# Two expert layers computed for the chosen experts alone, and attention worked in octets of half a sequence

## What is computed

```
x = x + 0.5 * ffn(LN(x))        # token-shift layer: mixes each row with the row before
x = x + attention(LN(x))        # 8 heads, softmax over 1024 keys, values wide
x = x + 0.5 * ffn(LN(x))
x = x + 0.5 * experts(LN(x))    # 16 experts, each token uses its best 2
x = x + linear_attention(LN(x)) # decaying state, scanned over the sequence
x = x + 0.5 * experts(LN(x))    # same weights again
```

```
probs = softmax(x_flat @ Wr + br)
topk_w, topk_idx = top_k(probs, 2);  topk_w /= sum(topk_w)
h   = x_flat @ W1[e] + b1[e]                      # 128 -> 128, for each expert e
h   = gelu(layernorm(h) * g1[e] + be1[e])
out = h @ W2[e] + b2[e]                           # 128 -> 128
y   = sum over the two chosen experts of topk_w * out
```

## Time and profile before

| | us |
|---|---|
| median of three runs | 894.28 |
| span of the profiled execution | 895.7 |
| PE busy (matmul) | 757.8 (85%) |
| DVE busy | 755.3 (84%) |
| ACT busy | 480.5 (54%) |
| POOL busy | 271.6 (30%) |

### The profile page before, as it was taken

The page is one execution under the profiler, slowest core; times in us unless marked ns, Lnnn a source line. Parts: engine busy times, 40 slices in busy tenths (PEclk is TensorE's granted clock), DMA queues, the critical chain, the costliest instruction groups (busy, mean ns, idle before and its releaser), DMA issues.

```text
span 895.7 us, 12505 instructions
## 1 busy us (share of the span) xinstructions
PE 757.8 (85%) x4069; PEld 408.9 (46%) x4074; DVE 755.3 (84%) x1697; ACT 480.5 (54%) x1245; POOL 271.6 (30%) x229
## 2 busy tenths in 40 slices
PE   4846889999999988998989896846989989989966
PEld 2523112232322333556656566624543556656656
DVE  7996799888887558799999999578764898999995
ACT  1424005767676876765766563335116765667742
POOL 4020000000000001234455456655000244456557
PEclk7788557999999998998999999976997999999998
DMA  7006860000000000000000000000000000000000
GB/s 235 1 3 138 179 104 2 1 1 2 1 1 2 1 0 1 1 1 1 1 0 2 0 1 1 1 1 0 2 1 1 0 2 12 1 1 13 1 12 13
DMA packets 11793, 16.66 MB, mean 19 GB/s; under 512 B 1456, under 2 KB 5584, under 8 KB 11728
## 3 DMA queue, kind: packets, MB, share of 16 engines
q1 hardware_dynamic: 11728, 15.86, 7.7%
HBM read 11.55 MB, written 4.19 MB: 18 GB/s over the span
## 4 chain that ended last, share of the span: by engine, by line
DVE 37%; PE 17%; issue 7%; ACT 6%; POOL 3%; POOLq 0%; DVEq 0%; ACTq 0%
DVE arena L1010 7%; DVE arena L994 6%; DVE small L206 6%; PE ps L854 3%; DVE arena L206 3%; POOL x L1089 3%; DVE small L202 3%; ACT arena L695 2%; PE ps L876 2%; DVE arena L1327 2%; PE ps L1209 1%; PE ps L579 1%; PE ps L1140 1%; DVE stat L215 1%; PE ps L853 1%
## 5 line engine op out<-in xcount | busy, mean ns | idle before, releaser
L1089 POOL TENSOR_TENSOR x<-x,arena 128x512 f32<-128x512 f32 x136 | 208.8, 1535 | 291.5 <-DVE arena L1010 288.0
L695 ACT ACTIVATE arena<-ps 128x512 f32<-128x512 f32 x256 | 132.4, 606 | 101.9 <-PE ps L568 101.7
L629 DVE TENSOR_REDUCE arena<-ps 128x1 f32<-128x512 f32 x256 | 159.5, 681 | 23.6 <-PE ps L549 23.0
L876 PE MATMUL ps<-w,arena 128*128 128x128 f32 x1024 | 141.1, 282 | 13.7 <-DVE arena L1010 9.2
L854 PE MATMUL ps<-w,xt 128*128 128x512 f32 x256 | 151.5, 675 | 0.0
L930 ACT ACTIVATE arena<-ps 128x512 f32<-128x512 f32 x128 | 76.4, 597 | 126.8 <-PE ps L854 107.7
L876 PEld LDWEIGHTS ps<-w,arena 128*128 128x128 f32 x1024 | 127.8, 196 | 18.5 <-ACT arena L968 10.0
L549 PE MATMUL ps<-arena 96*128 96x512 bf16 x256 | 112.3, 451 | 12.3 <-DMA arena<-att_parts 10.7
L968 ACT ACTIVATE arena<-ps,w 128x512 f32<-128x512 f32 x128 | 101.2, 791 | 31.5 <-PE ps L864 31.4
L864 PEld LDWEIGHTS ps<-cst,arena 128*128 128x128 f32 x512 | 63.4, 144 | 90.3 <-issue 45.4
L864 PE MATMUL ps<-cst,arena 128*128 128x128 f32 x512 | 80.2, 280 | 28.1 <-DVE arena L994 27.9
(11 more groups left out here) (181 smaller groups left out, 958.2 us busy)
## 6 DMA issues: line engine op xcount, KB each, us to landing
arena<-att_parts SPq DMA_DIRECT2D x28, 128.0 KB, 8.2
att_parts<-arena SPq DMA_DIRECT2D x12, 256.0 KB
arena<-att_parts SPq DMA_DIRECT2D x4, 384.0 KB, 8.8
x<-in_x SPq DMA_DIRECT2D x4, 256.0 KB, 3.5
arena<-att_parts SPq DMA_DIRECT2D x4, 256.0 KB, 9.4
out_x<-x SPq DMA_DIRECT2D x4, 256.0 KB, 2.3
w<-in_wpack SPq DMA_DIRECT2D x1, 611.0 KB, 5.8
row<-in_rows SPq DMA_DIRECT2D x1, 592.0 KB, 8.0
```

Of the source, the lines that this page charges most:

```text
L629: nc.vector.tensor_reduce(a_nm[:, hd % 2, k % 2, k // 2:k // 2 + 1], ps[:, RING_BANKS[u % 3], :], AX.X, ALU.max, negate=True).then_inc(a.m ...
L695: nc.scalar.activation(a_p[:, v % 8, half * 512:(half + 1) * 512], ps[:, score_bank(unit), :], ACT.Exp, scale=0.25).then_inc(a.ex, 1)
L876: ins = pe.matmul(ps[:, 4 + v % 2, j * P:(j + 1) * P], m_a[:, u % 4, j * P:(j + 1) * P], w2[:, 4 * (s % 4) + e, :], start=True, stop=True)
L1089: nc.gpsimd.tensor_tensor(xq, xq, m_tmp[:, v % 4, :].rearrange("p (j o) -> p j o", j=4), ALU.add)\
```

## The change

- **Expert layers.** The dense layer is replaced. Per half: DVE finds for each row its two experts as before, counts with two PE products and running sums how many rows go to each expert, and gives every (row, choice) a slot in a table of rows sorted by expert, each expert's part rounded up to whole tiles of 128 rows. With 2048 (row, choice) pairs in 16 experts, 31 tiles (NTL) always suffice, and 31 are always computed. POOL scatters the normalised rows into that table in DRAM with 16 indirect transfers of 128 rows; SP loads the table back in 8 groups of up to four tiles (31 = 7 x 4 + 3); each tile is transposed, multiplied with its expert's W1, scaled, transposed, passed through gelu and multiplied with W2, where the weights' address comes from a register that PE loads from a table of tiles; ACT starts the transfers of the results to DRAM; POOL gathers them back with 16 indirect transfers of 128 rows per half; DVE adds them to x with the gates.
- Biases go through DRAM (`bias_parts`), one more indirect transfer per half and three by SP; SP clears the two tables during attention.
- **Attention by octets.** An octet is a quad's four heads for half of the queries; the order of the ring, the maxima, the transfers of them (four per octet, 32 in all, 16 before) and the outputs go by octet. 42 ring units precede the first score.
- The norm statistics of the ffn layer of half 0 go between the ring's units in attention.
- PE runs products of zeros (`keep_clock`) while DVE routes.

```
-        RING_FIRST = turn_at[3] + 1 + 4
-        RING_SLOTS = 190
+        for o in range(NO):
+            for k in range(32):
+                ring.append(("mp", o, k))
+                if k == TURN_AFTER and o:
+                    ring.append(("turn", o - 1, 0))
...
+        RING_FIRST = turn_at[0] + 4
+        RING_OVER = 212
...
+            for o in range(first, last):
+                b, h0, half = octet(o)
+                sp.wait_ge(a.mpu, turn_at[o] + 1)
+                for k in range(NQ):
+                    sp.dma_start(a_qs[96:99, b, h0 + k, 512 * half:512 * (half + 1)].rearrange("i (j s) -> i j s", j=4),
+                                 a_nmt[12 * k:12 * k + 12, o % 2, :]).then_inc(a.nmrow[o], 16)
...
+            def scores(n):
+                o, i, h4 = n // 32, n % 32 // 4, n % 4
+                b, h0, half = octet(o)
+                if n % 32 == 0:
+                    pe.wait_ge(a.nmrow[o], 16 * NQ)
...
+        NTL = 2 * S // P + NE - 1
+        NGR = (NTL + 3) // 4
+        LEAD = 3
...
+        def moe_vector_slots(dve, vs, m):
...
+            yield vs.mark(nc.vector.tensor_tensor_scan(r_run[:, 8:8 + P], ps[:, bank, P:2 * P], zerof[:, 0:P], 0.0,
+                                                       ALU.add, ALU.add))
+            yield vs.mark(nc.vector.scalar_tensor_tensor(out=r_n, in0=ends, scalar=P - 1.0, in1=before, op0=ALU.add,
+                                                         op1=ALU.subtract))
...
+            nc.vector.tensor_copy(r_slot[b], r_slotf).then_inc(m.slot, 1)
...
+        def moe_pool_send(pool, m):
...
+            pool.wait_ge(m.slot, m.i + 1)
+            pool.wait_ge(s_clean, 32 * B)
+            for k in range(2):
+                for j in range(TB):
+                    pool.indirect_dma_start(
+                        out=rows_in[b], out_offset=bass.IndirectOffsetOnAxis(ap=r_slot[b][:, k * TB + j:k * TB + j + 1], axis=0),
+                        in_=xl[:, TB * b + j, :], in_offset=None).then_inc(m.sent, 16)
+                if k == 0:
+                    moe_pool_bias(pool, m)
...
+        def moe_pool_fetch(pool, m):
+            b, i = m.b, m.i
+            for k in range(4):
+                pool.wait_ge(t.ys[k], 16 * 2 * (i + 1))
+            for q in range(4):
...
+                for j in (2 * q, 2 * q + 1):
+                    for k in range(2):
+                        pool.indirect_dma_start(
+                            out=t_yg[:, b, k, j, :], out_offset=None, in_=rows_out[b],
+                            in_offset=bass.IndirectOffsetOnAxis(ap=r_slot[b][:, k * TB + j:k * TB + j + 1], axis=0))\
+                            .then_inc(t.yg[q], 16)
...
+        def moe_sync_load(sp, m, g):
+            b, u = m.b, NGR * m.i + g
+            if g == 0:
+                sp.wait_ge(m.sent, m.all_sent)
...
+            def hidden(u):
+                m, g = pair[(u - u0) // NGR], (u - u0) % NGR
...
+                regs = [pe.alloc_register(f"e{u}_{j}") for j in range(4)]
+                pe.load(regs, r_tab[m.b][0:1, 4 * g:4 * g + 4])
+                at = [pe.snap(r, min_val=0, max_val=(NE - 1) * P) for r in regs]
...
+                pe.matmul(ps[:, bank, :], pick[:, g, :], brow[:, m.b, :, 0, :], start=True, stop=False)
+                for j in range(k):
+                    ins = pe.matmul(ps[:, bank, j * P:(j + 1) * P], t_xt[:, u % 2, j * P:(j + 1) * P],
+                                    w1[:, :, :].rearrange("c e f -> c (e f)")[:, bass.ds(at[j], P)], start=False, stop=(j == k - 1))
...
+            routed(pair[0])
+            turn_in(u0)
+            for u in range(u0, u0 + LEAD):
+                turn_in(u + 1)
+                hidden(u)
+                between(u - u0)
+            routed(pair[1])
+            for u in range(u0, last):
+                turn(u)
+                if u + LEAD + 1 < last:
+                    turn_in(u + LEAD + 1)
+                if u + LEAD < last:
+                    hidden(u + LEAD)
+                out(u)
...
+            for u in range(u0, last):
+                gelu(u)
+                if u > u0:
+                    store(u - 1)
+                if u + LEAD + 1 < last:
+                    rows(u + LEAD + 1)
+                if u + LEAD < last:
+                    squares(u + LEAD)
+                out_in(u)
+            store(last - 1)
...
+            for u in range(u0, u0 + 2 * NGR, 2):
+                summed(u)
+                summed(u + 1)
+                dve.wait_ge(t.sqr, u + 2)
+                vs.finish(Chain(rstds(u + 1)))
+                scaled(u)
+                scaled(u + 1)
+                behind(u - u0)
...
+            vs.finish_both(norms, Chain(moe_vector_gap(dve, vs, m3[0])))
+            ffn_vector_mix(dve, vs, n2, f2, 1)
+            vs.finish(Chain(moe_vector_slots(dve, vs, m3[0])))
+            ffn_vector_add(dve, vs, f2, 1)
+            vs.finish(Chain(norm_vector_stats(dve, vs, n3, 1, False)))
+            vs.finish(Chain(moe_vector_gap(dve, vs, m3[1])))
+            vs.finish(Chain(moe_vector_slots(dve, vs, m3[1])))
...
+            moe_vector_tiles(dve, vs, m3, behind_m3)
```

More of the change, by code:

```diff
@@ L161, in finish, with finish_both @@
                     pass
+            def finish_both(self, one, other):
+                ended = [False, False]
+                while not all(ended):
+                    for i, chain in enumerate((one, other)):
+                        ended[i] = ended[i] or self.advance(chain)
         class Chain:
@@ new lines, in values @@
+            def values(step):
+                o, i = step // 8, step % 8
+                b, h0, half = octet(o)
+                if i == 0 and o >= 2:
+                    pe.wait_ge(a.done, o - 1)
+                pe.wait_ge(a.ex, 4 * step + 4)
+                for h4 in range(4):
+                    ins = pe.matmul(ps[32 * h4:32 * h4 + 32, 4 + half, :], a_v[:, TB * b + i, h0 + h4, :],
+                                    a_p[:, (4 * step + h4) % 16, :], start=(i == 0), stop=(i == 7))
+                ins.then_inc(a.av, 1)
@@ L664, in att_vector @@
[L664 to L676 removed]
+                    between(dve, u)
@@ L710, in att_pool_negmax @@
+            between(act, NSC)
+        def att_pool_negmax(pool, gs):
+            for o in range(NO):
+                pool.wait_ge(a.mn, o + 1)
+                if o >= 2:
+                    pool.wait_ge(a.mp, turn_at[o - 2] + 1)
+                nm, r1 = a_nmj[:, :, :], a_nmr[:, :, :]
+                parts = a_nmb[:, o % 2, :].rearrange("p (h i j) -> p i h j", h=NQ, i=3)
                 gs.step(nc.gpsimd.tensor_copy(parts[:, 0, :], nm))
@@ new lines, in build, with __init__ @@
+        HIDDEN_BANKS = (2, 3, 4, 5)
+        TURN_BANK, OUT_BANK = 6, 7
+        LOGIT_BANKS, COUNT_BANKS = (0, 6), (1, 7)
+        FILL_BANK = 2
+        class Moe:
+            logits, gap, gate = sem("e_logits"), sem("e_logit_gap"), sem("e_gate")
+            hot, count = sem("e_one_hot"), sem("e_counts")
+            base, slot, tab = sem("e_bases"), sem("e_slots"), sem("e_tile_table")
+            turned, pick = sem("e_bases_turned"), sem("e_tile_one_hot")
+            tix = sem("e_tile_experts")
+            got, rows_got = [sem(f"e_bias_rows{b}") for b in range(B)], [sem(f"e_bias_rows_in{b}") for b in range(B)]
+            gs, gsel = sem("e_scales_summed"), sem("e_scales_in")
+            rows_sent = [sem(f"e_rows_sent{b}") for b in range(B)]
+            added = sem("e_x_added")
+            def __init__(self, i, b, n):
+                self.i, self.b, self.n = i, b, n
+                self.sent, self.bias, self.brow = self.rows_sent[b], self.got[b], self.rows_got[b]
+                self.turn = i // B + 1
+                self.all_sent = 16 * 2 * TB * (i // B + 1)
```

1124 lines of the change are left out of this document (593 added, 531 removed).

## The result

The changed kernel took 800.84 us (median of 5 runs, 798.84 to 806.52) where the kernel before took 894.28 beside it: a ratio of 0.893, 95% interval 0.887 to 0.898. It is faster, as forecast, but by 93 us instead of 182, and outside the range that ended at 782. The profiled execution has a span of 804.7 us.

A forecast was written before the change was run, and what follows sets the result against it. Bound: DVE (92%, 86% busy) and PE (88% each) in the two expert stages. x complete 329 + first expert layer 145.3 + linear attention 97 + second expert layer 141.7 = 713, against the median 712 us; range 650 to 782.

The forecast's parts named there:

- PE's loop starts at T + 53.5: First expert layer: after routing, half 0's scatter and the first pair's sums, PE's tile loop starts 53.5 us after T.
- 47.9: Second expert layer: logits, routing, scatter and load 38.7 us, filling the pipeline 9.2; tiles start at L + 47.9.
- half 0's gathers hide under half 1's tiles: First expert layer: POOL's gathers of half 0 cost no time of their own; only half 1's, 17.6 us, are exposed.
- (1): Rival, expert layers: DVE holds POOL up, c = 1.9; +32 first layer, +33 second, 776 us; chance 0.15.
- (2): Rival, tile loops: register loads or address-dependent products break PE's queue, g = 5.7, +48, 760 us; chance 0.15.
- (3): Rival: lighter than reckoned, c = 0.7, g = 3.6, no row waits in attention, -53, 659 us; chance 0.19.
- g: PE's time per group of four tiles in the loops: 4.2 us, ends 3.6 (-19) and 5.3 (+35).
- c: POOL's time per indirect transfer in the expert layers: 1.1 us, bounds 0.70 and 1.91.
- (4): Rival: POOL's indirect transfers make it slower than before, from 3.9 us each; 970 at 5 us each; chance 0.03.
- Store's landing: End of the tile loops: last copy, issue and landing take 3.5 us before POOL gathers half 1.
- Attention: First score 122.5, 0.71 us per score, row waits 13.8, ring's end 293, tail 36; x complete at 329, 6 gained.
- (5): Rival, second layer: zero products, 36 at 0.42, 15 us, outlast the waits; +7, 719 us; counted in the forecast's 0.48.

The follow-up runs named there:

- r3: The changed kernel, unchanged, run on chip 2: 720.94 us, 0.803 of the kernel before.
- e1: The changed kernel without the 64 indirect transfers that carry rows to their slots (tiles computed on zeros), on chip 2: 721.3 us.
- p1: The changed kernel without its zero products on PE beside POOL's row transfers in the routings, on chip 2: 723.4 us.
- r1: The changed kernel, unchanged, run again on chip 1: 798.66 us, 0.892 of the kernel before.
- s1: The changed kernel, unchanged, run on chip 11 beside three cut versions: 795.0 us.
- r2: The changed kernel with half 0's gathers delayed until all groups of both halves are stored, on chip 1: 806.43 us, 0.902 of the kernel before.
- s3: The changed kernel with POOL's 64 indirect row transfers cut to 16-byte rows (tiles computed on zeros), on chip 11: 797.3 us.

## Why the prediction failed, point by point

The changed kernel on chip 2 (r3) shows what the forecast would have been worth without the waits. Times of stages from both profiles, T and L being x complete and linear attention's end; the last line is the profiled span:

| step | forecast | r3, chip 2 | after, with waits |
|---|---|---|---|
| x complete, T | 329 | 331.3 | 336.2 |
| PE's loop starts | T + 53.5 | T + 55.2 | T + 77.8 |
| last group stored (its issue) | T + 120.7 | T + 119.8 | T + 158.5 |
| linear attention starts | T + 145.3 | T + 145.2 | T + 184.0 |
| its length | 97 | 99.2 | 100.3 |
| PE's loop starts | L + 47.9 | L + 51.5 | L + 74.5 |
| end | L + 141.7 | L + 144.8 | L + 184.2 |
| span | 713 | 720.5 | 804.7 |

The two starts of the loop and the stages of r3, from its trace:

```profile
386.55 0.63 PE L1054 MATMUL ps<-cst,arena 128*128 128x128 f32 x4 [1.76 <-DVE arena L1170]
...
627.22 1.09 PE L1054 MATMUL ps<-cst,arena 128*128 128x128 f32 x4 [2.38 <-DVE arena L1170]
```

```profile
331.30:476.50 145.20, 115.38 (x621) 82.21 (x623) 91.66 (x345) 62.69 (x142) 66.99 (x67) 0.82 0.31 87
476.50:575.70 99.20, 68.10 (x514) 42.17 (x517) 74.17 (x161) 29.77 (x53) 29.55 (x16) 0.81 0.00 1
575.70:720.50 144.80, 89.38 (x518) 64.93 (x517) 71.73 (x273) 53.32 (x123) 63.34 (x66) 0.77 0.33 95
```

- **The step that failed** is one the prediction made without a word: that PE, ACT and DVE work beside POOL's indirect transfers as if these were not there. It is the overlap in "PE's loop starts at T + 53.5", in "47.9", in "half 0's gathers hide under half 1's tiles" and in "POOL's scatter of half 1 hides". After against r3: loop starts 22.6 and 23.0 us later, loops (first turned group to last store) 80.8 and 80.2 us instead of 64.6 and 63.7. That is 78.3 of the 84.2 us between the two spans. Leaving out the scatters on chip 11 gave back 43.6 (shown); the gathers' 28 to 30 compare two chips. One of the prediction's own signs of being wrong came true: the second layer's loop started at L + 74.5, much later than 48. Why some chips or occasions have the waits stays open.
- **Rivals.** None had this mechanism. (1) had it the wrong way round: DVE was to hold POOL up, and it is POOL's transfers that hold the others up. They take 0.96 us beside DVE's routing, 1.14 to 1.25 beside its 128x512 additions at 357 to 359, and 0.94 to 0.95 in the last burst. (Its +32 for the first layer adds up to 30 by its own terms.) The page of the Trainium skill (SBUF — State Buffer, A bandwidth-pool intuition that's wrong) has a transfer described by POOL take some 3100 ns beside a DVE copy. Nothing of that size shows here, but no long copy of DVE ran beside a transfer, so the page's own case wasn't met. (2) is wrong: on chip 2 nothing in the loop breaks PE's queue until the last groups, where PE waits for ACT. (3)'s g = 3.6 came true, its c = 0.7 didn't. (4) had the right suspicion, that what POOL issues is dear, but put the price into POOL's own time.
- **c**, an indirect transfer: 1.26 and 1.25, forecast 1.1, inside its bounds (0.70 to 1.91). It costs 17 x 0.16 = 2.7 more for the scatter ahead of the second loop and 2.4 for each last gather.
- **g**, a group: 3.6 to 3.7 instead of 4.2, and its terms were wrong both ways. In r3's row of 425.6 to 429.3 the products alone fill the 3.7, where I had 3.1, and the register load and ACT's handing over, 1.1 in my sum, add nothing to be seen. It should have given 8 us back a layer; r3's first loop, 64.6 from first group to last store against the 67.2 forecast, keeps only 2.6 of it. I take the rest to be the filling and emptying of the pipeline; at the end PE waits 1.2 to 1.7 us a group for ACT.
- **Store's landing**: 3.5 forecast. From the last store's issue to the second layer's first gather it is 4.8 (775.16 to 779.92); half 1's first gather in the first layer comes 2.9 behind the store.
- **Attention** is right in its sum and wrong in a term. The rows' waits were to be 13.8; after the first score's 3.25, PE's row has four of 3.5 us in all, near the low bound. The ring still ends at 294.0 against 293. The pace took up the rest: from the first score to the ring's end 171.1 us for 212 scores, 0.81 each, where I had 0.71 from one pair of rows, 6 us for turned outputs and the clock, and the 13.8. The tail took 42 instead of 36 in the profiled run, at a clock of 0.90; in r3 the ring ends at 291.5 and the tail takes 39.8 at 0.98, so the tail was some 4 too short in the sum even at the full clock.
- **Products of zeros** (5): the 36 ahead of the second loop, forecast as 15 us, take 9.6 in r3 and end 0.9 us before the first rows are turned (614.9 against 615.8), so they don't outlast the scatter. Taking away scatter or zeros alone moves the start little on chip 2 (from L to the gelu table load 48.8 us in e1, 50.9 in p1, 50.2 in r3), so both ends lie near each other, as the rival said, but the start is not late by its 7.

## What to carry to other kernels

When work is moved onto a path that the trace of before never uses, ask not only what the new operation costs its own engine but what it does to the semaphores of the others, and give that a rival with a price; here it was most of the error (78 of 88 us). After the change, compare each "remote" wait with the end of the instruction that should have released it, and lay the bursts of POOL's transfers beside them: the kind of burst is found in a minute. And before explaining a difference, run the unchanged kernel on the same chip: 720.9 and 798.7 us for one program were both true.

## What the runs showed of the hardware

- Of the chips that the results name, 0 and 2 have no "remote" waits (12 profiles), 1 and 11 have them in all six taken there (changed kernel 720.9 against 798.7 and 795.0 us), while the kernel before takes 893.6 to 897.4 on all four. Chips 0, 1 and 11 were used on one occasion each.
- In the profile after, whose result names no chip, in a burst of some 17 indirect transfers, each about 0.96 us of POOL and 1.26 apart, what PE releases reaches ACT or DVE 3 to 10 us late, and in a burst of 34 transfers 21.5 late. The engines' idle times there, 13.3 for DVE and 33.3 for ACT, are 13.0 and 33.0 in r1 (chip 1) and 10.6 and 32.9 in s1 (chip 11). The three waits of 6.1, 10.4 and 21.5 us end 3.6 to 6.5 us after the last transfer of their burst starts. Every "remote" wait of these traces is for PE or PE's own, but in r2's burst of 32 gathers DVE's waits for its own last step also grow, from too little to be listed to 1.23 us.
- An indirect transfer of 128 rows takes POOL 0.98 us on average with 512-byte rows (after) and with 16-byte rows (s3), and one of the 32 rows of biases 0.94 and 0.91: nearly all of it is a fixed cost.
